# Pair sums by accumulating DMAs, all tap weights on GpSimd, the convolution on four array tiles

## The chip, the cores and the metric

The kernel runs on one core of a Trainium2 chip. The metric is device time in microseconds: 101.33 us before, the median of three runs (101.04 to 101.79). The five engines of a core are named as the profile names them: PE (TensorE, with PEld for its weight loads), DVE (VectorE), ACT (ScalarE), POOL (GpSimd) and SP (SyncE, which here only issues DMAs).

## What is computed

A deformable attention over four images of 64 channels and 32x32 pixels, then a binarized 3x3 convolution with batch norm, residual and PReLU:

```python
x = _L0_conv_ref(x, ...)   # deformable attention, + q
x = _L1_conv_ref(x, ...)   # binary convolution
# _L0: per pixel 8 heads x 4 points; attn = softmax(q @ W_attn + b_attn)
#      loc = ref + off / norm; bilinear samples of v = q @ W_value + b_value at loc
#      out = (sampled * attn).sum(points) @ W_out + b_out + q
# _L1: s = sign(x + move0); y = conv3x3(s, scale * sign(w)), scale = mean|w| per output channel
#      y = batchnorm(y) + x + move1; y = where(y >= 0, y, a*y) + move2
```

## The kernel before

The partition dimension holds two images of 64 channels (128 rows), and there are two such groups, `g` = 0 and 1. The pixels are split into an upper and a lower half (`yh`) of 512 pixels each. No gather is done. Each sampling point is near its own pixel, so the attention is a sum over 4x4 taps: for each of the 16 taps of each half (32 taps, `t` = 0..31; four taps of one vertical offset make a row, 8 rows), three engines work one after another:

- the weight of the tap, `ay * hat` (128x512): DVE makes it at L822 into `a`, or POOL at L738 into `ap`. `DVE_COLUMNS` says how many taps of a row are DVE's: 2 in row 0, 1 in every other row. DVE makes `ay` of a row in PSUM (`attend`, L813, behind taps 1, 3, 6, 10, 14, 18 and 22), and ACT copies it to SBUF (`copy_ay`, L611) for POOL, after DVE's own weight of that row is made.
- PE spreads the weight over channels (`spread(t)`, L420: four 64x64 tiles, f32, into one of two PSUM pairs). `spread(t)` waits for `product(t-2)`.
- DVE multiplies it with the shifted values (`product(t)`, L837, 128x1024, into slot `t % 8` of `prod`).

PE then projects the products into the output accumulators (`project`, L440, a "unit"). Taps 2 and 3 of each row are a unit each. Taps 0 and 1 are first added by POOL (`pair_sum`, L746, into `sum2`), so a row has three units, and row n's are put behind the spreads of row n+1 (`UNITS_AFTER`); the sum of row n stands behind `spread(4n+6)`, only sum 0 and sum 3 a group or two otherwise. `carry_x` (L433) adds x to the accumulators, before row 0's units and, for the lower half, behind `spread(20)`.

At the end PE runs the convolution: `convolve_row` (L469) issues for each of the 9 kernel positions and each group one 128x128 bf16 matmul with a block-diagonal weight over 512 pixels. The first three positions of group 0 stand ahead of the last unit, the rest of the upper half behind it. Then PE reads the flag that says whether an offset was out of range (a fallback branch, not taken here) and runs `convolve_rest`, which waits for the signs (L668, ACT) of the lower half: one pixel row of the upper half (128x32 matmuls) and the nine positions of the lower half, for each group in turn. DVE takes the statistics of each of the four PSUM banks (L938), then come the small steps of batch norm and the final elementwise work and four output DMAs.

## Time and profile before

| | us |
|---|---|
| median of three runs | 101.33 |
| the profiled execution | 101.12 |
| its span, first to last instruction | 99.2 |
| first spread to last spread | 16.4 to 76.4 |
| convolution and what stands between its parts | 78.2 to 87.5 |
| statistics, batch norm, final work, output | 87.5 to 99.2 |

Busy shares of the span are PE 81%, DVE 70%, POOL 56%, ACT 46%. The granted TensorE clock is at its full level until the convolution ends. A busy share is an average over these stages; so each stage is read by itself, from who waits for whom. Matmuls of different tiles start a few ns apart and overlap, so a group of four f32 matmuls on four tiles (8 records, since f32 takes two passes) shows about 1.06 us in the timeline but the next group starts 0.86 us after it.

### The profile page before, as it was taken

The numbers are of one execution on the slowest core, as the hardware profiler recorded it, in microseconds if no ns is written. First come the engines' busy times: TensorE is split into PE (matmuls) and PEld (weight loads), VectorE is DVE, ScalarE is ACT, GpSimd is POOL, SyncE is SP. The second block draws the span as 40 slices with busy tenths as digits, with TensorE's granted clock in tenths as the row PEclk, the third lists the DMA queues.
The fourth block names the chain that finished last, engine by engine and source line by source line (L and its number), as shares of the span: only waits on it lengthen the run. The fifth ranks groups of instructions, "written<-read, shape, count | busy, mean of one in ns | idle before, by whom it ended". The sixth has DMA issues, their size and how long they took to land.

```text
span 99.2 us, 1591 instructions
## 1 busy us (share of the span) xinstructions
PE 80.8 (81%) x598; PEld 32.7 (33%) x598; DVE 69.6 (70%) x89; ACT 45.8 (46%) x73; POOL 55.6 (56%) x42
## 2 busy tenths in 40 slices
PE   5999798698999785979979799979999999950000
PEld 4554281112344232324233345424242234420000
DVE  1405869989989930997994984998876434548990
ACT  3101999947999920099815590050000064003960
POOL 7950000189950899999999985984949000000600
PEclk9999999999999999999999999999999999999555
DMA  2997000000000000000000000000000000000055
GB/s 52 224 363 275 1 0 0 0 7 0 0 0 0 0 7 0 0 0 0 7 0 0 0 7 0 0 3 0 0 7 0 0 0 7 0 0 3 0 217 206
DMA packets 2169, 3.43 MB, mean 35 GB/s; under 512 B 368, under 2 KB 880, under 8 KB 2160
## 3 DMA queue, kind: packets, MB, share of 16 engines
q1 hardware_dynamic: 1872, 2.89, 8.5%
q10 hardware_dynamic: 288, 0.43, 1.8%
q8 instruction: 5, 0.08, 0.3%
q14 instruction: 4, 0.03, 0.1%
HBM read 2.27 MB, written 1.05 MB: 33 GB/s over the span
## 4 chain that ended last, share of the span: by engine, by line
PE 44%; issue 15%; ACT 13%; POOL 12%; DVE 12%; ACTq 1%; DVEq 0%; POOLq 0%
PE banks L420 14%; PE banks L440 11%; PE banks L469 8%; POOL ap L738 7%; DVE prod L837 5%; POOL sum L746 5%; ACT tab L599 4%; ACT hat L604 3%; PE banks L487 3%; DVE banks L813 2%; ACT prod L717 2%; PE banks L393 2%; PE banks L433 2%; PE banks L385 2%; ACT prod L719 1%
## 5 line engine op out<-in xcount | busy, mean ns | idle before, releaser
L837 DVE TENSOR_TENSOR prod<-banks,vpad 128x1024 f32<-128x1024 f32 (+1 forms) x33 | 38.5, 1186 | 11.2 <-PE banks L420 11.1
L738 POOL TENSOR_TENSOR ap<-ays,hat 128x512 f32<-128x512 f32 x23 | 28.9, 1290 | 13.7 <-ACT ays L611 13.7
L420 PE MATMUL banks<-ap,cst 64*64 64x512 f32 x184 | 26.0, 599 | 3.6 <-POOL ap L738 1.8
L746 POOL TENSOR_TENSOR sum<-prod 128x1024 f32<-128x1024 f32 x8 | 19.0, 2376 | 4.6 <-DVE prod L837 4.6
L440 PE MATMUL banks<-prod,wo 64*64 64x512 f32 x128 | 17.7, 591 | 0.0
L420 PEld LDWEIGHTS banks<-ap,cst 64*64 64x64 f32 x184 | 7.5, 132 | 16.4 <-issue 9.1
L611 ACT ACTIVATE ays<-banks 128x512 f32<-128x512 f32 x8 | 4.7, 592 | 15.0 <-DVE a L822 15.0
L420 PE MATMUL banks<-a,cst 64*64 64x512 f32 x72 | 10.2, 602 | 1.1 <-DVE prod L837 0.6
L770 POOL TENSOR_SCALAR prod<-prod,prm,st 128x512 f32<-128x512 f32 x2 | 1.5, 776 | 15.1 <-ACT st L711 15.1
L599 ACT ACTIVATE tab<-u,cst 128x1024 f32<-128x1024 f32 x8 | 8.9, 1141 | 0.2
L440 PE MATMUL banks<-sum,wo 64*64 64x512 f32 x64 | 9.0, 589 | 0.0
L440 PEld LDWEIGHTS banks<-prod,wo 64*64 64x64 f32 x128 | 6.0, 133 | 7.7 <-issue 7.1
L469 PE MATMUL banks<-sg,wcb 128*128 128x512 bf16 (+2 forms) x42 | 8.4, 352 | 0.0
L604 ACT ACTIVATE hat<-tab 128x1024 f32<-128x1024 f32 x8 | 8.3, 1047 | 0.1
L668 ACT ACTIVATE sg<-banks,st 128x512 bf16<-128x512 f32 x2 | 1.3, 688 | 14.3 <-PE banks L440 14.3
L822 DVE TENSOR_TENSOR a<-banks,hat 128x512 f32<-128x512 f32 x9 | 6.2, 692 | 0.3
L813 DVE TENSOR_TENSOR banks<-banks,hat 128x512 f32<-128x512 f32 x8 | 5.5, 691 | 0.8 <-PE banks L408 0.8
L469 PEld LDWEIGHTS banks<-sg,wcb 128*128 128x128 bf16 x42 | 3.5, 97 | 5.5 <-issue 1.6
L938 DVE BATCH_NORM_STATS2 bns<-banks 128x6 f32<-128x512 f32 x4 | 2.7, 695 | 3.3 <-PE banks L469 3.3
L420 PEld LDWEIGHTS banks<-a,cst 64*64 64x64 f32 x72 | 2.4, 131 | 7.3 <-issue 5.1
L440 PEld LDWEIGHTS banks<-sum,wo 64*64 64x64 f32 x64 | 3.0, 133 | 4.0 <-issue 3.4
L393 PEld LDWEIGHTS banks<-win,xs 128*128 128x128 f32 x32 | 3.8, 191 | 1.1 <-issue 1.1
(80 smaller groups left out, 83.1 us busy)
## 6 DMA issues: line engine op xcount, KB each, us to landing
out_dram<-prod SPq DMA_DIRECT2D x4, 256.0 KB, 2.1
xs<-x_dram SPq DMA_DIRECT2D x3, 256.0 KB, 5.1
wcf<-w_conv_dram SPq DMA_DIRECT2D x1, 288.0 KB, 5.4
wab<-w_abs_dram SPq DMA_DIRECT2D x1, 288.0 KB, 5.1
xs<-x_dram ACTq DMA_DIRECT2D x1, 256.0 KB, 4.0
cst<-const_dram SPq DMA_DIRECT2D x1, 227.0 KB, 5.3
win<-w_in_dram ACTq DMA_DIRECT2D x1, 160.0 KB, 2.6
cst<-const_dram SPq DMA_DIRECT2D x1, 128.0 KB, 5.7
```

What stands on the lines that cost most here:

```text
L393: mm = pe.matmul(ps_log[yh][:, at:at + C], xs[:, g, q:q + P], wp[:, 2, :], start=False, stop=(n == NCH - 1 and g == G - 1), skip_group_che ...
L420: mm = pe.matmul(ps_w[t % 2][rows_out, g, :], sel_of(g)[rows_in, rows_out], weights_at(t)[rows_in], start=True, stop=True)
L440: mm = pe.matmul(ps_out[g][rows_out], wo[rows_in, rows_in], source[rows_in, g, :], start=False, stop=last, skip_group_check=True)
L469: mm = pe.matmul(ps_y[yh][g][:, first_row * W:last_row * W], wcb[:, ky * K + kx, :], sg[:, g, y0:y0 + last_row - first_row, kx:kx + W], st ...
L599: nc.scalar.activation(tab[:, n % 2], u[:, :, yh, :], ACT.Abs, bias=cst[:, c_tap + k:c_tap + k + 1]).then_inc(s_abs, 1)
L604: nc.scalar.activation(hat[:, yh, :, k, :], tab[:, n % 2], ACT.Relu, bias=1.0, scale=-1.0).then_inc(s_hat, 1)
L611: nc.scalar.activation(ays[:, n % RY, :], ps_ay[:], ACT.Identity).then_inc(s_ayc, 1)
L738: pool.tensor_tensor(ap[:, j % RAP, :], ays[:, t // TAPS % RY, :], hat[:, yh, 0, kx, :], ALU.mult).then_inc(s_ap, 1)
L746: pool.tensor_tensor(sum2[:, n % NS], prod[:, t % PR], prod[:, (t + 1) % PR], ALU.add).then_inc(s_s2, 1)
L813: nc.vector.tensor_tensor(ps_ay[:], ps_att[:], hat[:, yh, 1, ORDER[row], :], ALU.mult).then_inc(s_ay, 1)
L822: nc.vector.tensor_tensor(a[:, i % RA, :], ps_ay[:], hat[:, yh, 0, kx, :], ALU.mult).then_inc(s_a, 1)
L837: nc.vector.tensor_tensor(by_half_row(prod[:, t % PR, g, :]), by_half_row(ps_w[t % 2][:, g, :]), v_window(g, yh, ky, kx), ALU.mult).then_i ...
```

## The change

- `DVE_COLUMNS` becomes 2 for row 0 and 0 for the others: POOL makes 30 weights rather than 23, DVE two rather than nine. `copy_ay` waits only for `attend`.
- `sum2` is gone. For rows 0 to 6 POOL issues a DMA that adds `prod` slot t+1 onto slot t (`accum_op=ALU.add`, 512 KB, SBUF to SBUF), with one semaphore for even and one for odd rows. The unit "sum n" waits for that DMA and reads the slot itself. `product(t+8)` for column 0 now waits until that unit is projected, for column 1 until the DMA has landed. Row 7 has no sum: its four taps are four units.
- `softmax_sum(1)` and `softmax_recip(1)` move from behind products 5 and 6 to behind products 3 and 4.
- `convolve_row` issues, for each position, four 64x64 bf16 matmuls on the four quadrants of the array (two images of each group at once), each with the 64x64 weight. `wcb` is 128x9x64, written by one activation rather than two, and its memset is gone. The two images of group 1 come out swapped, so its residual `x1` is stored swapped (four 64-partition copies on ACT), and each of its two output chunks is stored by two DMAs. Statistics of both groups wait for one semaphore per half.

```diff
-SUMMED = range(ROWS)
-DVE_COLUMNS = [2] + [1] * (ROWS - 1)
+SUMMED = range(ROWS - 1)
+DVE_COLUMNS = [2] + [0] * (ROWS - 1)
...
                 if kind == "sum":
-                    pe.wait_ge(s_s2, n + 1)
-                    source = sum2[:, n % NS]
+                    pe.wait_ge(s_s2[n % 2], 16 * (n // 2 + 1))
+                    source = prod[:, TAPS * n % PR]
...
-                    mm = pe.matmul(ps_y[yh][g][:, first_row * W:last_row * W], wcb[:, ky * K + kx, :],
-                                   sg[:, g, y0:y0 + last_row - first_row, kx:kx + W], start=(ky == 0 and kx == 0),
-                                   stop=(ky == K - 1 and kx == K - 1 and last_row == RH), skip_group_check=True)
+                    for g in range(G):
+                        for i in range(PAIR):
+                            rows_in, rows_out = quadrant(i, g)
+                            mm = pe.matmul(ps_y[yh][g][rows_out, first_row * W:last_row * W], wcb[rows_in, ky * K + kx, :],
+                                           sg[rows_in, g, y0:y0 + last_row - first_row, kx:kx + W], start=(ky == 0 and kx == 0),
+                                           stop=(ky == K - 1 and kx == K - 1 and last_row == RH), skip_group_check=True)
...
-            for g in range(G):
-                act.wait_ge(s_acc, UPPER_UNITS)
-                nc.scalar.activation(chunk(x1, g, 0), ps_out[g][:], ACT.Identity, bias=prm[:, p_bo:p_bo + 1]).then_inc(s_x1, 1)
-            act.wait_ge(s_zero, 4)
+            act.wait_ge(s_acc, UPPER_UNITS)
+            nc.scalar.activation(x1n[:], ps_out[1][:], ACT.Identity, bias=prm[:, p_bo:p_bo + 1]).then_inc(s_x1, 1)
+            nc.scalar.activation(chunk(x1, 0, 0), ps_out[0][:], ACT.Identity, bias=prm[:, p_bo:p_bo + 1]).then_inc(s_x1, 1)
+            act.wait_ge(s_zero, 3)
...
-                if n >= NS:
-                    pool.wait_ge(s_acc, units_done(("sum", n - NS)))
-                pool.tensor_tensor(sum2[:, n % NS], prod[:, t % PR], prod[:, (t + 1) % PR], ALU.add).then_inc(s_s2, 1)
+                pool.dma_start(prod[:, t % PR], prod[:, (t + 1) % PR], accum_op=ALU.add).then_inc(s_s2[n % 2], 16)
...
             for n in range(ROWS - 1):
-                weight(TAPS * (n + 1) + 1)
-                if n:
-                    pair_sum(n)
-                weight(TAPS * (n + 1) + 2)
-                weight(TAPS * (n + 1) + 3)
-                if n == 0:
-                    pair_sum(0)
+                for column in range(TAPS):
+                    weight(TAPS * (n + 1) + column)
+                    if column == 1:
+                        pair_sum(n)
...
-            pair_sum(ROWS - 1)
-
...
+                if t == 3:
+                    softmax_sum(1)
+                if t == 4:
+                    softmax_recip(1)
                 if t in ROW_AFTER:
                     n = ROW_AFTER.index(t) + 1
                     attend(n)
-                    weight(TAPS * n)
-                if t == 5:
-                    softmax_sum(1)
-                if t == 6:
-                    softmax_recip(1)
```

On POOL, at the start of the tap loop, these rows stood before (the products of the second half's softmax are `prob`; `sum` is the pair sum, `ap` the tap weights):

```order
L738 TENSOR_TENSOR ap<-ays,hat 128x512 x5
L746 TENSOR_TENSOR sum<-prod 128x1024
L760 TENSOR_TENSOR prob<-ex,lrec 128x512
L738 TENSOR_TENSOR ap<-ays,hat 128x512
L746 TENSOR_TENSOR sum<-prod 128x1024
L738 TENSOR_TENSOR ap<-ays,hat 128x512 x3
```

and these stand there now:

```order
L754 TENSOR_TENSOR ap<-ays,hat 128x512 x4
L760 DMA prod<-prod 128x1024
L754 TENSOR_TENSOR ap<-ays,hat 128x512 x2
L771 TENSOR_TENSOR prob<-ex,lrec 128x512
L754 TENSOR_TENSOR ap<-ays,hat 128x512 x2
L760 DMA prod<-prod 128x1024
L754 TENSOR_TENSOR ap<-ays,hat 128x512 x4
```

Each row of taps has four weights and a DMA where it had three weights and an add, and the first DMA is issued after four weights rather than five.

On PE, from the spread of tap 31 to the read of the flag, these rows stood before:

```order
L420 MATMUL banks<-ap,cst 64x512 x4
L440 MATMUL banks<-prod,wo 64x512 x4
L440 MATMUL banks<-sum,wo 64x512 x4
L469 MATMUL banks<-sg,wcb 128x512 x3
L440 MATMUL banks<-prod,wo 64x512 x4
L469 MATMUL banks<-sg,wcb 128x512 x3
L469 MATMUL banks<-sg,wcb 128x480 x3
L469 MATMUL banks<-sg,wcb 128x512 x6
L469 MATMUL banks<-sg,wcb 128x480 x3
L545 TENSOR_LOAD flagi
```

and these stand there now:

```order
L431 MATMUL banks<-ap,cst 64x512 x4
L451 MATMUL banks<-prod,wo 64x512 x12
L483 MATMUL banks<-sg,wcb 64x512 x12
L451 MATMUL banks<-prod,wo 64x512 x4
L483 MATMUL banks<-sg,wcb 64x512 x12
L483 MATMUL banks<-sg,wcb 64x480 x12
L556 TENSOR_LOAD flagi
```

Ahead of the convolution's first part stand three units (12 matmuls) rather than two. That part is three positions of both groups in 12 small matmuls, and behind the last unit 24 small matmuls stand where there were 15 large ones.

## Rows read from the trace of the kernel before

**Rows 1.** Timeline of PE, 33 to 76 us: start us, us, engine, line, operation [idle <-releaser].
```profile
33.07 1.11 PE L440 MATMUL banks<-prod,wo 64*64 64x512 f32 x6
35.00 1.09 PE L420 MATMUL banks<-ap,cst 64*64 64x512 f32 x8 [0.82 <-POOL ap L738]
...
38.53 1.09 PE L420 MATMUL banks<-ap,cst 64*64 64x512 f32 x8 [1.00 <-POOL ap L738]
...
43.59 1.09 PE L420 MATMUL banks<-ap,cst 64*64 64x512 f32 x8 [0.52 <-DVE prod L837]
44.47 1.07 PE L440 MATMUL banks<-prod,wo 64*64 64x512 f32 x8
45.33 1.07 PE L420 MATMUL banks<-ap,cst 64*64 64x512 f32 x8
...
75.52 1.04 PE L420 MATMUL banks<-ap,cst 64*64 64x512 f32 x8
```

**Rows 2.** Busy time by stretch: us, PE, PEld, DVE, ACT, POOL busy (x), PEclk, DMA.
```profile
35.00:75.70 40.70, 37.52 (x330) 14.65 (x334) 30.79 (x30) 13.77 (x31) 36.14 (x24) 1.00 0.01 2
```

**Rows 3.** Timeline of DVE around `attend` and the weight of a row.
```profile
40.90 0.69 DVE L813 TENSOR_TENSOR banks<-banks,hat 128x512 f32<-128x512 f32 x1
41.63 0.69 DVE L822 TENSOR_TENSOR a<-banks,hat 128x512 f32<-128x512 f32 x1
42.23 2.35 DVE L837 TENSOR_TENSOR prod<-banks,vpad 128x1024 f32<-128x1024 f32 x2
44.84 1.22 DVE L837 TENSOR_TENSOR prod<-banks,vpad 128x1024 f32<-128x1024 f32 x1 [0.26 <-PE banks L420]
```

**Rows 4.** Timeline of POOL, four places of the tap loop.
```profile
22.51 3.75 POOL L738 TENSOR_TENSOR ap<-ays,hat 128x512 f32<-128x512 f32 x3 [0.47 <-ACT ays L611]
...
32.60 1.10 POOL L760 TENSOR_TENSOR prob<-ex,lrec 128x512 f32<-128x512 f32 x1 [4.00 <-DVE lrec L791]
33.67 1.28 POOL L738 TENSOR_TENSOR ap<-ays,hat 128x512 f32<-128x512 f32 x1
...
60.63 2.36 POOL L746 TENSOR_TENSOR sum<-prod 128x1024 f32<-128x1024 f32 x1 [1.53 <-DVE prod L837]
```

**Rows 5.** Costliest groups: busy us, mean ns of one, idle before and its releaser.
```profile
L738 POOL TENSOR_TENSOR ap<-ays,hat 128x512 f32<-128x512 f32 x23 | 28.9, 1290 | 13.7 <-ACT ays L611 13.7
L746 POOL TENSOR_TENSOR sum<-prod 128x1024 f32<-128x1024 f32 x8 | 19.0, 2376 | 4.6 <-DVE prod L837 4.6
L611 ACT ACTIVATE ays<-banks 128x512 f32<-128x512 f32 x8 | 4.7, 592 | 15.0 <-DVE a L822 15.0
```

**Rows 6.** DMA queue of the loads and stores (packets, MB, share), and the output's issues.
```profile
q1 hardware_dynamic: 1872, 2.89, 8.5%
...
out_dram<-prod SPq DMA_DIRECT2D x4, 256.0 KB, 2.1
```

**Rows 7.** SP's DMA issues in the timeline: start us, us on SP, line, tensors, count.
```profile
3.06 0.43 SPq L359 DMA_DIRECT2D wo<-w_out_dram  x1
...
94.49 2.65 SPq L366 DMA_DIRECT2D out_dram<-prod  x4
```

**Rows 8.** The chain that ended last, from the convolution on: start us, us, what.
```profile
78.28 0.77 PE banks L469 x3
79.05 1.02 PE banks L440 x8
80.06 7.46 PE banks L469 x39
...
87.55 0.71 DVE bns L938
...
88.29 0.28 DVE mv L940
```

**Rows 9.** ACT's signs of the lower half, in its timeline.
```profile
80.16 1.27 ACT L668 ACTIVATE sg<-banks,st 128x512 bf16<-128x512 f32 x2 [14.33 <-PE banks L440]
```

**Rows 10.** By source line: PE's sequencer reads the flag, then goes on after the branch.
```profile
L545 PEldq TENSOR_LOAD <-flagi x1: 483/483/483, 80.0 to 80.0; - x1
...
L576 PEldq EVENT_SEMAPHORE  x1: 51/51/51, 81.3 to 81.3; - x1
```

**Rows 11.** Convolution alone, by stretch: us, PE busy (x), PEld busy (x), PEclk, DMA.
```profile
83.20:83.32 0.12, 0.12 (x5) 0.09 (x4) 1.00 0.00 0
```

More of the change, by code:

```diff
@@ L328, in units_of @@
             if n == ROWS - 1:
-                return [("tap", first + 2), ("sum", n), ("tap", first + 3)]
+                return [("tap", t) for t in range(first, first + TAPS)]
             return [("tap", first + 2), ("tap", first + 3), ("sum", n)]
         UNITS_AFTER = {6: [("tap", 2), ("tap", 3)], 7: [("sum", 0)], 17: [("tap", 15), ("sum", 3)], 18: [], 20: [],
-                       21: [("tap", 18), ("tap", 19)]}
+                       21: [("tap", 18), ("tap", 19)], 31: [("tap", 28), ("tap", 29)]}
         for n in range(2, ROWS):
@@ L568, in _ @@
                 pe.wait_ge(s_gs, 4)
[L569 to L571 removed]
+                for ky in range(K):
+                    convolve_above(ky)
             pe.end_ifs()
             pe.wait_ge(s_p, products_done(NT * YH - 1, G - 1))
[L575 to L577 removed]
+            pe.wait_ge(s_sg, 4)
+            convolve_rest()
             pe.wait_ge(s_mv, 1)
@@ L606, in copy_ay @@
             def copy_ay(n):
-                act.wait_ge(s_a, sum(DVE_COLUMNS[:n + 1]))
+                act.wait_ge(s_ay, n + 1)
+                if n == 0:
+                    act.wait_ge(s_a, DVE_COLUMNS[0])
                 if n >= RY:
@@ L693, in _ @@
                 sign(g, 1, ps_out[g][:], st[:, 16:17], s_sg)
+            for i in range(PAIR):
+                rows_in, rows_out = quadrant(i, 1)
+                nc.scalar.activation(chunk(x1, 1, 1)[rows_out], ps_out[1][rows_in], ACT.Identity,
+                                     bias=prm[rows_in, p_bo:p_bo + 1]).then_inc(s_x1swap, 1)
             act.wait_ge(s_flag, 1)
@@ L726, in _ @@
             pool.memset(vpad[:].rearrange("p g y a x -> p (g y a x)"), 0.0).then_inc(s_zero, 1)
-            pool.memset(wcb[:].rearrange("p k c -> p (k c)"), 0.0).then_inc(s_zero, 1)
             pool.memset(sg[:].rearrange("p g y x -> p (g y x)"), 0.0).then_inc(s_zero, 1)
@@ L877, in _ @@
             nc.vector.tensor_scalar(flagi[:], flag[:, 0:1], 0.0, None, ALU.is_gt).then_inc(s_flag, 1)
-            for g in range(G):
-                dve.wait_ge(s_sg, G + g + 1)
-                nc.vector.tensor_scalar(chunk(x1, g, 1), ps_out[g][:], prm[:, p_bo:p_bo + 1], None, ALU.add).then_inc(s_x1low, 1)
+            dve.wait_ge(s_sg, G + 1)
+            nc.vector.tensor_scalar(chunk(x1, 0, 1), ps_out[0][:], prm[:, p_bo:p_bo + 1], None, ALU.add).then_inc(s_x1low, 1)
             dve.wait_ge(s_flag, 1)
@@ L932, in _ @@
                         residual_of(yh, g, ps_gout[yh][g], s_gx)
+                dve.wait_ge(s_gx, 4)
+                dve.wait_ge(s_x1low, 1)
+                dve.wait_ge(s_x1swap, 4)
+                nc.vector.tensor_copy(x1[:, 0, :], gacc[:, 0, :]).then_inc(s_gn, 1)
+                for i in range(PAIR):
+                    rows_in, rows_out = quadrant(i, 1)
+                    nc.vector.tensor_copy(x1[rows_out, 1, :], gacc[rows_in, 1, :]).then_inc(s_gn, 1)
+                dve.wait_ge(s_gn, 3)
             dve.end_ifs()
             for n in range(G * YH):
-                g, yh = divmod(n, YH)
-                dve.wait_ge(s_y, n + 1)
+                yh, g = divmod(n, G)
+                dve.wait_ge(s_y, yh + 1)
                 nc.vector.bn_stats(bns[:, n, :], ps_y[yh][g][:]).then_inc(s_bns, 1)
```

92 lines of the change are left out of this document (50 added, 42 removed).

## The prediction

> **What bounds the kernel now.** I read the chain that ended last first, then the timelines of PE, DVE and POOL side by side. The chain runs through PE for most of its length, but in the tap loop it hops to DVE and POOL wherever PE waited. A group of four f32 matmuls starts 0.86 us after the one before it when nothing holds it (44.47 to 45.33 in [rows 1]). Between spread 9 (35.00) and spread 31 (75.52) the program has 39 such groups (22 spreads, 17 units), 1.72 for the carry of x, 0.62 for the transposes of the second softmax and 0.12 for the flag's matmul: 39 x 0.86 + 2.46 = 36.0 us of the 40.5. So 4.5 us are waits of PE. Twice it waits for a POOL weight (0.82 and 1.00 [rows 1]); four times (43.59 and three like it) it waits 0.5 to 0.6 for a product. The cause of the second kind is in [rows 3]: product 11 stands behind `attend` and DVE's own weight, 42.23 rather than 40.90. The cause of the first kind is in [rows 4]: POOL stood idle 4.00 us for the reciprocal and then had an add to do. Over the loop POOL is busy 36.1 of 40.7 us [rows 2], nearly as full as PE.
>
> **The tap loop up to spread 9.** POOL ends weight 3 at 22.0 as before. It then makes weights 4 and 5 (1.24 each: three in 3.75 [rows 4]), issues the first DMA at 24.5 and pays D for it, makes 6 and 7, `prob` (1.07) and 8 and 9. With D = 1.2, weight 9 is there at 31.8 instead of 34.95, the reciprocal having moved ahead. PE ends its previous group at 33.07 + 0.43 = 33.5 [rows 1], and the lower positions on ACT start 0.7 sooner since the copy of `ay` no longer waits for a DVE weight [rows 5]; spread 9 starts at about 33.4: **1.6 us sooner**.
>
> **From spread 9 to spread 31.** DVE loses seven weights; between product 10 and 11 there is `attend` alone, 0.62 us less. A spread must follow its predecessor but one by 1.24 to the product's start, 1.23 for the product and 0.13 back to PE, 2.60 in all, against 2.58 for three PE groups, so small waits stay: I take 0.28 a row, five rows, 1.4. That gives 33.4 + 36.0 + 1.4 = 70.8 for spread 31, **3.1 us more** on top, 4.7 in all. POOL's share: 22 weights and six DMA issues, 22 x 1.24 + 6D = 34.5 at D = 1.2, under 37.4, and it keeps ahead as far as the four weight buffers let it.
>
> **The accumulating DMA.** No row has one. Call T the time from POOL reaching it to its landing. It needs the product of column 1, thus about 2.5 us after that tap's spread (1.24 + 1.23 + 0.07), and the sum's unit stands ten groups behind that spread (8.6, and 0.3 of waits): T up to 6.4 costs nothing. Three places are tighter: sum 0 (issued 24.5, wanted 30.8: 6.3), sum 1 (issued 31.8 behind `prob`, wanted 36.8: 5.0), and sum 3, which stands one spread nearer (about 5.0 after POOL's issue). Stepping through the rows, the loop's end moves by 2(T - 5.0), and above 6.3 by another (T - 6.3), since then every row pays and each stall is half absorbed by the next. Bounds of T: the load and store queue moved 2.89 MB in 8.5% of 16 engines' span, 21.4 GB/s each, 343 together [rows 6]: 1.53 us for 512 KB in one pass, 3.06 if the destination is read besides. The output's 256 KB land 2.1 us after issue, 0.76 of it transfer [rows 6], so 1.35 is fixed. For D, an issue on SP holds it 0.43 [rows 7], the lower end, and I bound it above by the add it replaces, 2.37 [rows 5]. T lies between 0.43 + 1.35 + 1.53 = 3.3 and 2.37 + 1.35 + 4.6 = 8.3 (three passes). I take two passes and D = 1.2, between its ends: T = 5.6, which costs 1.2. Loop: 4.7 - 1.2 = **3.5 us gained**. The other bounds: 4.7, or with 8.3 a loss of 3.9.
>
> The Trainium skill (DMA: Bandwidth & Descriptors, "Anatomy of one DMA") fits a GpSimd-issued DMA by 2.0 us plus bytes over 436 GB/s, 3.2 us here; no run here shows one yet. By that alone the DMA would cost nothing and the total would be 1.2 us lower than mine.
>
> **The convolution and what leads to it.** Count from the end of spread 31, before at 76.38. Before: two units, three matmuls, the last unit ending 3.7 later (80.06), signs ready 1.37 after that [rows 9], the remaining 39 matmuls until 87.5, statistics until 88.3 [rows 8]: 11.9. After: three units (2.58), a switch (0.11), three positions, the last unit (1.09 to its end). The term to size is p, the time of a position in four small matmuls. A large matmul of 512 columns takes 0.215 (36 of about full length and six short ones in 0.77 + 7.46 us [rows 8]) and before a position takes two of them, 0.43. Four tiles at once take 0.215 if their matmuls overlap as those of L420 do. The upper bound is issue: that is eight instructions per position, and the f32 groups sustain 16 in 0.86, 0.43 per eight, without showing that they could go faster. Against that bound: five matmuls and four weight loads of 128x32 fit in 0.12 us [rows 11], so what is already queued runs faster than that. I take p = 0.27. Then the last unit ends at 2.58 + 0.11 + 0.81 + 1.09 = 4.6. The signs are ready at 6.0. The flag's read began when the remaining matmuls began, and the sequencer went on 1.29 later [rows 10]; with 24 small ones to hand out, partly ahead, I expect it 2.4 after the unit, 7.0. The rest is 12 short matmuls and nine positions, 0.6 + 2.4 = 3.0: 10.0. Now both lower banks end together, so two statistics of 0.65 stand behind, not one, and with the steps between the aggregate starts at 11.4 rather than 11.9: **0.5 us gained**. Ends: p = 0.215 with the signs as the limit (start at 5.9, 2.3 for the rest), 2.3 gained; p = 0.43 with everything bound by issue (last unit at 5.1, 2.6 to hand out the upper rest, about 1.1 for the branch, 48 pairs of 0.107, statistics), 15.3, 3.4 lost.
>
> **What costs nothing.** ACT's four swap copies (0.6 each): the upper two stand ahead of `copy_ay(6)`, whose weights are wanted over 5 us later; the lower two end 2.6 after the last unit, before batch norm wants them at about 7. If that cover went, each would cost its 0.6. The two extra output DMAs take 0.43 of SP each; the four chunks are issued in 2.65, 0.74 apart [rows 7], so a second half can push the next chunk by 0.1, and the last chunk, a single DMA with the widest gap ahead, is not delayed. The wcb memset and one activation go from engines that wait there.
>
> **The sum.** 3.5 + 0.5 = 4.0. The profiled execution took 101.12 (span 99.2 and 1.92 around it), 0.2 under the median: 101.12 - 4.0 = **97.1 us**.
>
> **Rivals.**
> - *The DMA lands late (slower).* T of 7.1 eats the gains of loop and tail (2 x 2.1 + 0.8 = 5.0, against 4.7 + 0.5), so from about 7.2 it decides; at 8.3 the loop loses 3.9, and 101.1 + 3.9 - 0.5 = **104.5**. For it: an addition has to read what it writes, and the queue's measured 21 GB/s an engine leaves 3.1 us for that alone. Against: it needs a third pass or a D of 2.4 besides.
> - *POOL becomes the bound.* If issuing takes D = 2.4, what the add took, POOL has 27.3 + 14.4 = 41.7 us between spread 9 and 31, and the DMA still has T over 5.2. That is 4.3 more than 37.4, and 1.2 more than the 40.5 of before: the loop keeps 0.4 of its 1.6 + 3.1, and with the tail's 0.5 the time is **100.2 us**. For it: POOL was busy 89% of the loop. Against: an issue on SP takes a sixth of it.
> - *The convolution is bound by issue.* The instruction count doubles for the same work. With p = 0.43 the tail loses 3.4: 101.1 - 3.5 + 3.4 = **101.0**, no change. For: nothing in the trace shows a faster sustained hand-out. The Trainium skill (TensorE: Matmul & The Clock Gate, Part 1) says the sequencer may spend about 62 ns per matmul and then binds once the array work per matmul is shorter; here that would be 53 ns, p = 0.25 if weight loads came free and 0.5 if they cost the same. The f32 groups' 107 ns per pair rules out the latter, and no row settles the former.
>
> **Chances.** The forecast, with T under 6.2 and p under 0.35: 0.50, its own range 94.1 (T = 5, p = 0.215) to 98.7. Late DMA 0.24. POOL bound 0.12. Issue bound 0.14. A change of 1% (about what a measurement here can tell) is 1.0 us. Faster: the forecast, half of the issue bound's (where p is short of 0.43) and half of POOL's: 0.63. Same: the other halves, 0.13. Slower: the late DMA's, 0.24. Range: 94.2 at the lower end; above, 103.0 leaves out half of the late DMA's chance.
>
> **What would show it.** Spread 31 starts near 72.0; before spread 9 no wait for POOL; PE's idle before L451 of a sum unit is under 1 us in total (if each row shows a wait for a DMA, the first rival); POOL's gap around its DMA issue is about 1.2; positions of L483 come 0.27 apart. The prediction is wrong if sum units wait every row, if weights on POOL are late again, or if the matmuls of L483 come one by one at over 0.1 us.

## The result, and the profile after

The changed kernel takes **95.68 us** (median of four runs, 95.59 to 96.38) against 101.19 for the kernel before on the same chip: ratio 0.9461, 95% interval 0.94 to 0.9521, so 5.5 us less. The prediction was 97.1, range 94.2 to 103.0. Medians here are over all executions of a kernel, and ratios leave out those more than 1.5% longer than its fastest. The profiled execution has a span of 93.9 us against 99.2.

Read the stages one by one. PE's timeline of the changed kernel (start us, us, engine, line, operation, count, idle before and who ended it); compare [rows 1] and [rows 8]:

```profile
16.69 1.09 PE L431 MATMUL banks<-a,cst 64*64 64x512 f32 x8 [0.29 <-DVE a L831]
...
33.35 1.34 PE L431 MATMUL banks<-ap,cst 64*64 64x512 f32 x8
...
52.19 1.09 PE L431 MATMUL banks<-ap,cst 64*64 64x512 f32 x8 [1.07 <-DVE prod L850]
...
71.42 1.04 PE L431 MATMUL banks<-ap,cst 64*64 64x512 f32 x8
72.28 2.76 PE L451 MATMUL banks<-prod,wo 64*64 64x512 f32 x24
74.86 0.84 PE L483 MATMUL banks<-sg,wcb 64*64 64x512 bf16 x12
75.52 1.04 PE L451 MATMUL banks<-prod,wo 64*64 64x512 f32 x8
76.38 1.46 PE L483 MATMUL banks<-sg,wcb 64*64 64x512 bf16 x24
78.07 2.27 PE L483 MATMUL banks<-sg,wcb 64*64 64x32 bf16 x48 [0.23 <-ACT sg L680]
82.03 0.38 PE L590 MATMUL banks<-mv,cst 128*128 128x2 f32 x2 [1.69 <-DVE mv L959]
```

The rows give a ledger that is used for every kernel below: first spread; from the first to the last spread (**loop**); from the end of the last spread, 0.86 after its start, to the matmuls on the aggregate (**tail**); from there to the end of the span (**output**).

| us | before | changed | gain |
|---|---|---|---|
| first spread at | 16.36 | 16.69 | -0.33 |
| loop | 59.16 | 54.73 | 4.43 |
| tail | 12.23 | 9.75 | 2.48 |
| output | 10.59 | 11.87 | -1.28 |
| span | 99.2 | 93.9 | 5.3 |

So two stages gave more than forecast (4.43 and 2.48, for 3.5 and 0.5), and one that was to cost nothing lost 1.3.

Who waits, in the list of waits of the changed kernel (engine, line, for whom: us in total, times, longest):

```profile
DVE prod L850 <- PE banks L431: 11.7, 17, 1.9
PEld banks L451 <- DMA prod<-prod: 1.1, 2, 0.8
PE banks L431 <- DVE prod L850: 1.1, 1, 1.1
```

DVE now waits for PE, not the reverse; the one long wait of PE for a product is that of spread 20 (52.19). The page of the changed kernel: POOL's weights, its DMA issues, the queue that they feed (packets, MB, share of 16 engines), and their landing (KB each, median us from issue), beside the output's:

```profile
L754 POOL TENSOR_TENSOR ap<-ays,hat 128x512 f32<-128x512 f32 x30 | 40.4, 1564 | 17.4 <-ACT ays L623 15.7
...
L760 POOL DMA_DIRECT2D prod<-prod x7 | 7.5, 1077 | 0.4 <-issue 0.4
...
q0 software_dynamic: 1008, 3.67, 20.6%
...
prod<-prod POOLq DMA_DIRECT2D x7, 512.0 KB, 4.8
...
out_dram<-prod SPq DMA_DIRECT2D x4, 128.0 KB, 2.6
out_dram<-prod SPq DMA_DIRECT2D x2, 256.0 KB, 2.6
```

The accumulating DMA lands 4.8 us after its issue (4.5 to 5.1). It shows 1.08 us on POOL, but part of it overlaps the next operation:

```profile
31.60 1.11 POOL L760 DMA_DIRECT2D prod<-prod  x1
32.21 5.51 POOL L754 TENSOR_TENSOR ap<-ays,hat 128x512 f32<-128x512 f32 x4
```

Here the next weight starts 0.61 after the issue, and behind the first of the seven 0.77, so that is what POOL pays: about a quarter of the add's 2.37 [rows 5].

### The profile page after: what moved, and what is told of

The parts are those of the page before. It is cut to its first block, busy times and chain, and to the rows that moved or that the text cites. A ratio compares the mean times of both kernels' runs of the same rounds, so it can differ in the third digit from the quotient of the medians.

```text
span 93.9 us, 1689 instructions
## 1 busy us (share of the span) xinstructions
PE 76.6 (82%) x648; PEld 33.0 (35%) x648; DVE 65.0 (69%) x81; ACT 47.9 (51%) x76; POOL 51.0 (54%) x47
## 3 DMA queue, kind: packets, MB, share of 16 engines
q0 software_dynamic: 1008, 3.67, 20.6%
HBM read 2.27 MB, written 1.05 MB: 35 GB/s over the span
## 4 chain that ended last, share of the span: by engine, by line
PE 67%; ACT 15%; DVE 7%; issue 4%; POOL 3%; ACTq 1%; DVEq 0%; POOLq 0%
PE banks L431 27%; PE banks L451 23%; PE banks L444 4%; ACT tab L609 3%; ACT hat L614 3%; PE banks L483 3%; PE banks L501 3%; POOL ap L754 2%; ACT prod L734 2%; PE banks L404 2%; PE banks L396 2%; ACT prod L736 2%; DVE bns L957 1%; ACT sg L680 1%; ACT u L602 1%
## 5 line engine op out<-in xcount | busy, mean ns | idle before, releaser
L754 POOL TENSOR_TENSOR ap<-ays,hat 128x512 f32<-128x512 f32 x30 | 40.4, 1564 | 17.4 <-ACT ays L623 15.7
L850 DVE TENSOR_TENSOR prod<-banks,vpad 128x1024 f32<-128x1024 f32 (+1 forms) x33 | 38.6, 1187 | 11.7 <-PE banks L431 11.7
L431 PE MATMUL banks<-ap,cst 64*64 64x512 f32 x240 | 33.9, 596 | 1.3 <-DVE prod L850 1.1
L451 PE MATMUL banks<-prod,wo 64*64 64x512 f32 x200 | 27.8, 590 | 0.0
L451 PEld LDWEIGHTS banks<-prod,wo 64*64 64x64 f32 x200 | 9.9, 133 | 11.5 <-issue 9.6
L760 POOL DMA_DIRECT2D prod<-prod x7 | 7.5, 1077 | 0.4 <-issue 0.4
L483 PE MATMUL banks<-sg,wcb 64*64 64x512 bf16 (+2 forms) x84 | 4.6, 350 | 0.2 <-ACT sg L680 0.2
L390 PE MATMUL banks<-xs,win 128*64 128x512 f32 x16 | 4.1, 611 | 0.0
L404 PE MATMUL banks<-win,xs 128*128 128x64 f32 x32 | 4.0, 277 | 0.0
L444 PE MATMUL banks<-xs,cst 64*64 64x512 f32 x16 | 3.8, 590 | 0.0
L396 PE MATMUL banks<-prm,top_ones 128*128 128x512 f32 x4 | 3.0, 846 | 0.7 <-ACT u L602 0.7
```

The source lines that it names most:

```text
L404: mm = pe.matmul(ps_log[yh][:, at:at + C], xs[:, g, q:q + P], wp[:, 2, :], start=False, stop=(n == NCH - 1 and g == G - 1), skip_group_che ...
L431: mm = pe.matmul(ps_w[t % 2][rows_out, g, :], sel_of(g)[rows_in, rows_out], weights_at(t)[rows_in], start=True, stop=True)
L444: mm = pe.matmul(ps_out[g][rows_of_i], cst[rows_of_i, c_eye + i * C:c_eye + (i + 1) * C], chunk(xs, g, yh)[rows_of_i], start=True, stop=Fa ...
L451: mm = pe.matmul(ps_out[g][rows_out], wo[rows_in, rows_in], source[rows_in, g, :], start=False, stop=last, skip_group_check=True)
L483: mm = pe.matmul(ps_y[yh][g][rows_out, first_row * W:last_row * W], wcb[rows_in, ky * K + kx, :], sg[rows_in, g, y0:y0 + last_row - first_ ...
L754: pool.tensor_tensor(ap[:, j % RAP, :], ays[:, t // TAPS % RY, :], hat[:, yh, 0, kx, :], ALU.mult).then_inc(s_ap, 1)
```

## The experiments

### Do the parts add up?

**Convolution alone**: the kernel before with the second half of the change. Core of the edit (the loop over two halves is for the chunks of group 1):

```diff
-            def convolve_row(yh, g, ky, first_row, last_row):
+            def convolve_row(yh, ky, first_row, last_row):
+                    for g in range(G):
+                        for i in range(PAIR):
+                            rows_in, rows_out = quadrant(i, g)
...
-                sp.dma_start(chunk_of(out, g, yh), chunk(res, g, yh)).then_inc(s_done, 16)
+                    for i in range(PAIR):
+                        rows_in, rows_out = quadrant(i, g)
+                        sp.dma_start(chunk_of(out, g, yh)[rows_in], chunk(res, g, yh)[rows_out]).then_inc(s_done, 16)
```

> The kernel before with the convolution on four tiles, the swap copies and the six output DMAs alone; its loop (adds on GpSimd, DVE's own weight) is unchanged. From the two traces, counted from the end of spread 31, the aggregate matmul came 2.5 us sooner after the change and the stretch behind it took 1.25 us longer. Theory A (the parts add up, and the longer output stage belongs to the six output DMAs): spread 31 starts at 75.5, the convolution gains 2.5, the output loses 1.2, and the time is 101.2 - 1.3 = 99.9 us; issues of the output DMAs take about 0.58 on SP. Theory B (the longer issues come from the accumulating DMAs of the loop, which share the 16 engines and leave something behind): here, without them, issues take 0.34 as before, the output loses nothing and the time is 98.7. Theory C (the convolution only gained because the loop freed GpSimd and ACT before it): gain 0.5 or less, 100.7 or more.

**Loop alone**: the kernel before with the first half, which is the DMAs, the weights on POOL, row 7 unsummed and the earlier softmax steps.

```diff
-SUMMED = range(ROWS)
-DVE_COLUMNS = [2] + [1] * (ROWS - 1)
+SUMMED = range(ROWS - 1)
+DVE_COLUMNS = [2] + [0] * (ROWS - 1)
...
-                pool.tensor_tensor(sum2[:, n % NS], prod[:, t % PR], prod[:, (t + 1) % PR], ALU.add).then_inc(s_s2, 1)
+                pool.dma_start(prod[:, t % PR], prod[:, (t + 1) % PR], accum_op=ALU.add).then_inc(s_s2[n % 2], 16)
```

> The kernel before with the new loop alone: pair sums by accumulating DMAs, all four weights of a row on GpSimd, the softmax sum sooner; convolution and four output DMAs as before. Theory A (parts add up): spread 31 starts at 71.4 as in the changed kernel, the convolution takes 11.9 from the end of spread 31 to the aggregate as before, the output issues take 0.34 and the output stage is that of before: 101.2 - 4.1 = 97.1 us. Theory B (the accumulating DMAs lengthen the output issues): issues take 0.58 although there are only four, and the time is 97.7 to 98.3.

Measured: 99.67 us (ratio 0.9838, 0.9802 to 0.9874) and 98.24 us (0.970, 0.967 to 0.973). PE's timelines of the two, last spread and aggregate, first of the convolution alone, then of the loop alone:

```profile
75.86 1.04 PE L433 MATMUL banks<-ap,cst 64*64 64x512 f32 x8
...
85.61 0.38 PE L593 MATMUL banks<-mv,cst 128*128 128x2 f32 x2 [1.70 <-DVE mv L964]
```

```profile
71.09 1.04 PE L418 MATMUL banks<-ap,cst 64*64 64x512 f32 x8
...
85.02 0.38 PE L577 MATMUL banks<-mv,cst 128*128 128x2 f32 x2 [1.09 <-DVE mv L935]
```

| us | first spread | loop | tail | output | span |
|---|---|---|---|---|---|
| before | 16.36 | 59.16 | 12.23 | 10.59 | 99.2 |
| convolution alone | 16.69 | 59.17 | 8.89 | 12.19 | 97.8 |
| loop alone | 16.36 | 54.73 | 13.07 | 11.28 | 96.3 |
| changed | 16.69 | 54.73 | 9.75 | 11.87 | 93.9 |

The loop is the same to 0.01 us with either convolution, and the new convolution shortens the tail by 3.34 behind the old loop too, so the theory that it gained only through a freer loop falls. The tail shows something that my expectation for the loop alone forgot, though the prediction had counted it: the new loop leaves the last row unsummed, which puts one more unit, 0.86, behind the last spread. The unit takes 0.84 to 0.86 of the 3.34 (12.23 to 8.89) back. The longer output comes with the six output DMAs: it is there in the convolution alone, where no accumulating DMA exists. The loop alone has 0.7 more too, of another kind: SP issues its four in 0.33 to 0.35 us each, as before the change, so the time is in theory B's range, but not for its reason. Its DMA view over the last 5.4 us, GB/s in 40 equal slices:

```profile
GB/s 0 0 0 0 0 0 197 379 410 349 394 364 410 379 364 394 364 425 349 410 364 243 15 182 440 394 334 425 152 15 15 30 15 15 0 0 0 0 0 0
```

Behind the last full slice stand five of 15 to 30 GB/s, one or two packets of 2 KB per slice, as if a single engine ended about 0.6 after the others. An instruction load (one packet, 0.01 MB) goes through the engines in that stretch. It does so in the output stretch of the changed kernel and of the one with whole chunks (below) too, which have no such end, so it doesn't explain it. The cause stays open.

### Which half of the loop's change gives the gain?

**GpSimd adds**: all four weights on POOL, but the sums by POOL's add.

```diff
...
-                pool.dma_start(prod[:, t % PR], prod[:, (t + 1) % PR], accum_op=ALU.add).then_inc(s_s2[n % 2], 16)
+                pool.tensor_tensor(sum2[:, n % NS], prod[:, t % PR], prod[:, (t + 1) % PR], ALU.add).then_inc(s_s2, 1)
```

> The changed kernel with the pair sums made by GpSimd's add again (2.37 us each), and still all four weights of a row on GpSimd. Theory A (GpSimd becomes the bound): from spread 9 to spread 31 it has 22 weights of 1.24 and 6 adds of 2.37, 41.5 us against the 38.1 that this stretch took, and a later start of spread 9 by about 1; the time is 95.7 + 4 = 99.7 us, so that the move of the weights pays only with the DMAs. Theory B (GpSimd has enough slack from its four weight buffers): 96.5 us or less.

**DVE column**: sums by DMA, but the first weight of a row on DVE, behind `attend`.

```diff
-DVE_COLUMNS = [2] + [0] * (ROWS - 1)
+DVE_COLUMNS = [2] + [1] * (ROWS - 1)
...
-                for column in range(TAPS):
+                for column in range(1, TAPS):
                     weight(TAPS * (n + 1) + column)
...
                     attend(n)
+                    weight(TAPS * n)
```

> The changed kernel with the first weight of each row on DVE as before (0.62 us each, seven of them) and the pair sums by DMA. Theory A (DVE's own weight is what made PE wait 0.5 to 0.6 a row): those waits come back in five rows, spread 31 starts about 2 us later than 71.4, 97.6 us. Theory B (GpSimd's relief, 1.24 a row, gives as much as DVE's load takes, or PE's waits had another cause): 95.4 to 96.2 us.

Measured: 99.26 us (ratio 0.979, 0.9741 to 0.9838) and 98.75 us (0.9733, 0.9686 to 0.978). POOL in the first, busy us from spread 9 to spread 31 (us, PE, PEld, DVE, ACT, POOL, clock, DMA share, GB/s):

```profile
34.66:75.06 40.40, 37.73 (x330) 13.19 (x326) 28.50 (x27) 14.78 (x32) 39.80 (x28) 1.00 0.01 2
```

39.8 of 40.4: with the adds, POOL is the bound. In the second, POOL has time but PE waits for products again, as in [rows 1]; three of the rows:

```profile
42.03 1.09 PE L431 MATMUL banks<-ap,cst 64*64 64x512 f32 x8 [0.52 <-DVE prod L848]
...
48.83 1.09 PE L431 MATMUL banks<-ap,cst 64*64 64x512 f32 x8 [0.52 <-DVE prod L848]
...
53.99 1.09 PE L431 MATMUL banks<-a,cst 64*64 64x512 f32 x8 [0.64 <-DVE prod L848]
```

| loop, us | first weight of a row on DVE | on POOL |
|---|---|---|
| sums by POOL | 59.16 | 58.25 |
| sums by DMA | 57.05 | 54.73 |

The upper left cell is the kernel before. The three others also have the softmax steps moved ahead and row 7 unsummed, and no run has these alone, so neither 0.9 nor 2.1 is the worth of one edit. By stretch, the four kernels take from the first spread to spread 9: 18.64 (before), 17.85 (GpSimd adds), 17.39 (DVE column) and 16.66 (changed). From spread 9 to spread 31 they take 40.52, 40.40, 39.66 and 38.07. So nearly all of the 0.9 lies at the start of the loop, where POOL had stood idle for the reciprocal [rows 4], and may be the softmax's. If moving the softmax costs nothing, what is left behind spread 9 bounds the edits: the weights alone give at most 0.1, the DMAs alone at most 0.9, both 2.45, and at least 1.5 is there only with both. A kernel with the softmax steps alone would settle it. The DMA makes room on POOL, and the weights use it to unload DVE. I had expected 1.1 less for the kernel with DVE's column: the waits came back as said, 1.6 us between spread 9 and spread 31, but spread 9 itself also came 0.95 later (34.30), only 0.22 of that because of a later first spread.

### The accumulating DMA: what it costs, and how much slack it has

**Plain copy**: the addition is left out.

```diff
-                pool.dma_start(prod[:, t % PR], prod[:, (t + 1) % PR], accum_op=ALU.add).then_inc(s_s2[n % 2], 16)
+                pool.dma_start(prod[:, t % PR], prod[:, (t + 1) % PR]).then_inc(s_s2[n % 2], 16)
```

> The changed kernel with its seven DMAs as plain copies of the same 512 KB, so the addition of the pair is left out. In the changed kernel such a DMA landed 4.5 to 5.1 us after its issue, held GpSimd about 0.6 to 0.75, and kept each engine busy for 2.76 us (20.6% of 93.9 us over seven). Theory A (an accumulating DMA reads what it writes, so the copy makes one pass instead of two): the copy takes about 1.4 to 1.6 us of the engines, lands after 3.4 to 3.7, PE's waits for it (1.1 us in two places) go, and the time is about 0.5 to 1 us less, 94.7 to 95.2. Theory B (the time is the fixed cost of a DMA that GpSimd issues): lands after 4.5 and the time stays at 95.7.

**Pair later**: the issue stands one weight further back on POOL.

```diff
-                    if column == 1:
+                    if column == 2:
                         pair_sum(n)
```

> The changed kernel with each pair sum issued behind the row's third weight on GpSimd instead of behind the second, 1.24 us later; so it lands 1.24 later wherever GpSimd is not waiting anyway. Theory A (the slack as the prediction put it: a landing up to 5.0 costs nothing, beyond it 2 us per us, since two sums are tighter than the rest): with 4.8 + 1.24 = 6.0 the loop gets 2 us longer, 97.7, and PE waits for the DMA in two or three places only. Theory B (PE runs close behind the DMA in every row): the wait appears in all seven rows and costs 1 us each, 100 or more. Theory C (there is slack everywhere, and GpSimd gains from not waiting for the product): 95.4 to 96.0.

Measured: the copy 95.52 us (ratio 0.9404, 0.9376 to 0.9432), the later pair 98.33 us (0.9701, 0.9649 to 0.9754). The page of the copy, its queue and its landing:

```profile
q0 software_dynamic: 1008, 3.67, 9.7%
...
prod<-prod POOLq DMA_DIRECT2D x7, 512.0 KB, 2.9
```

For the same 512 KB the engines work 9.7% x 93.3 / 7 = 1.29 us a copy and 20.6% x 93.9 / 7 = 2.76 us an accumulation, and the landing goes from 2.9 to 4.8. So an accumulation costs the engines a little over twice the copy, as the prediction's second pass would. The Trainium skill (DMA: Bandwidth & Descriptors, "Anatomy of one DMA") gives 3.2 us for a GpSimd-issued DMA of this size; the copy's 2.9 is near it, the accumulation's 4.8 is not, so that fit does not hold for `accum_op`. And the 1.9 us are worth almost nothing here: the loop is 54.58 with the copy and 54.73 with the addition. The 1.1 us of waiting for the DMA in the list above are PEld's, whose weight loads run ahead of the matmuls; PE itself has no wait for a DMA. The one place where the matmuls are held back is the sum of row 3, the DMA that took 5.1 to land. The two units of that place, in the changed kernel and then with the copy:

```profile
47.34 2.07 PE L451 MATMUL banks<-prod,wo 64*64 64x512 f32 x16
```

```profile
47.00 1.93 PE L451 MATMUL banks<-prod,wo 64*64 64x512 f32 x16
```

The spread behind them starts 1.89 and 1.72 after their start, so the wait costs 0.17, which is the loop's 0.15. It isn't taken up by the next stall: the wait before spread 20 is 1.07 and 1.06.

Issued later, the same DMA costs 2.1 us: loop 56.83. The waits:

```profile
PEld banks L451 <- DMA prod<-prod: 5.3, 6, 1.7
...
PE banks L451 <- DMA prod<-prod: 1.6, 3, 0.8
```

and PE stops before three sums, 0.49, 0.79 (here) and 0.29 us:

```profile
49.87 1.09 PE L451 MATMUL banks<-prod,wo 64*64 64x512 f32 x8 [0.79 <-DMA prod<-prod]
```

With the issue 1.24 further back, T goes from 4.8 to about 6.0. The prediction's slack rule, nothing up to 5.0 and 2 us per us beyond, gives 2.1; measured 2.1 in the loop. (The profiled span rose 2.1 as well, the median time 2.65; no trace shows the other 0.5.) Theory A holds, and with it a warning: the change sits on the knee, with the sum of row 3 landing at 5.1 and already costing its 0.17.

### The wait before spread 20

**Sum of row 3 later**: a unit goes between spreads 18 and 19.

```diff
-        UNITS_AFTER = {6: [("tap", 2), ("tap", 3)], 7: [("sum", 0)], 17: [("tap", 15), ("sum", 3)], 18: [], 20: [],
+        UNITS_AFTER = {6: [("tap", 2), ("tap", 3)], 7: [("sum", 0)], 17: [("tap", 15)], 18: [("sum", 3)], 20: [],
```

> The changed kernel with one unit moved: the sum of row 3 is projected after spread 18 and not after spread 17. In the changed kernel three spreads (18, 19, 20) stood without a unit between 18 and 19 and after 20, and PE waited 1.07 us for DVE's product before spread 20 (52.19). Theory A (PE's order makes the stall: a spread must stand 2.6 us behind its predecessor but one, and two groups take 1.7): with the unit between, the wait goes and spread 31 starts 0.9 to 1.1 sooner, 94.7 us. Theory B (DVE is the limit over the loop, so a stall removed at one place returns at the next): gain below 0.3, 95.4 to 95.7.

Measured 95.21 us (ratio 0.9379, 0.9342 to 0.9415); spans 93.0, 92.6, 92.8, 92.8 against 93.9, 94.0, 93.8, 93.9. The same spread in PE's timeline:

```profile
51.38 1.09 PE L431 MATMUL banks<-ap,cst 64*64 64x512 f32 x8 [0.20 <-DVE prod L850]
```

The wait of 1.07 is 0.20, and the loop 53.71: 1.02 less. The wait was made by PE's order, and it didn't return elsewhere. The median time fell by only 0.47, since more of it lies outside the span (1.9 to 2.8 us a run, against 1.8 to 2.4 in the changed kernel); the intervals of the two ratios overlap, the spans don't.

### The output stage

Three kernels change who issues the output, one changes what is issued.

**Half on ACT**: SP issues one half of chunk (1,1), ACT the other. **Split chunk last**: the same, with the order of the last two chunks turned, so that ACT waits for the fourth result (`wait_ge(s_res, 4)`); the last two lines are its alone.

```diff
-                    for i in range(PAIR):
+                    for i in range(PAIR if n == 0 else 1):
...
+            act.wait_ge(s_res, 3)
+            rows_in, rows_out = quadrant(1, 1)
+            act.dma_start(chunk_of(out, 1, 1)[rows_in], chunk(res, 1, 1)[rows_out]).then_inc(s_done, 16)
...
-            return yh, G - 1 - k
+            return yh, G - 1 - k if yh == 0 else k
```

> The changed kernel with one of the six output DMAs (the second half of chunk (1,1)) issued by ACT, so that SP has five. In the changed kernel SP issued six DMAs back to back at 87.92, 88.49, 89.12, 89.75, 90.26 and 90.90, and the last was ready to go at about 90.24. Theory A (SP's queue of issues delays the last one): the last issue moves from 90.90 to about 90.3 and the time falls by 0.6, to 95.1. Theory B (the last landing is set by something else, 2.6 us after its issue rather than 2.1, since the small descriptors of the halves stand ahead of it in the same engines): the time falls by 0.2 or less.

> The changed kernel with the last two chunks of the result in the other order, so that the split chunk is last, and its two halves issued by SP and by ACT at the same time. Theory A (halves on two queues go through the 16 engines side by side and use all ports, so a split chunk costs what a whole one costs): whole chunk issued at about 89.8, halves both at about 90.3, last packet at about 92.5 instead of 93.17, time 95.0 us. Theory B (the engines work through one DMA after another, whichever queue): within 0.2 of the changed kernel, 95.5 to 95.9.

**Halves by GpSimd** (with the sum of row 3 later; SP leaves out the first split chunk):

```diff
+            pool.wait_ge(s_res, 1)
+            for i in range(PAIR):
+                rows_in, rows_out = quadrant(i, 1)
+                pool.dma_start(chunk_of(out, 1, 0)[rows_in], chunk(res, 1, 0)[rows_out]).then_inc(s_early, 16)
```

> The kernel with the sum of row 3 one spread later (95.2 us, span 92.6 to 93.0), and with the first split chunk of the output issued by GpSimd, which is idle by then, so that SP has four issues. Putting one half on ACT's queue brought 0.1 in one order of the chunks and cost 0.6 in another. Theory A (the six DMAs follow one another at about 0.7 us because of the hardware queue that SP feeds, and GpSimd's queue runs beside it): the whole chunk is issued at 87.8 rather than 88.3, the last packet comes 0.5 to 0.8 sooner, 94.5 us. Theory B (the 16 engines are shared and a half costs its 0.7 whoever issues it): 95.1 to 95.4. [...]

**Whole chunks**: each split chunk goes out in one DMA. It leaves out the exchange of the two images, so the images of group 1 stay swapped in the output.

```diff
-                    for i in range(PAIR):
-                        rows_in, rows_out = quadrant(i, g)
-                        sp.dma_start(chunk_of(out, g, yh)[rows_in], chunk(res, g, yh)[rows_out]).then_inc(s_done, 16)
+                    sp.dma_start(chunk_of(out, g, yh), chunk(res, g, yh)).then_inc(s_done, 16)
```

> The changed kernel with the chunks of the swapped images written by one DMA of 128 partitions each instead of two of 64, so four output DMAs; the exchange back of the two images of a pair is left out. In the kernel with the new loop alone the output DMAs were whole and SP issued them in 0.33 to 0.35 us each, in those with the new convolution in 0.47 to 0.60. With one of six moved to ACT the last issue on SP came 0.68 earlier and the last packet only 0.10 earlier, so the issue on SP is not what ends last; the packets of a half took 144 ns against 89. Theory A (a DMA over half the partitions is slow in itself, in issue and per packet): with whole DMAs the issues return to 0.34, from the first issue to the end it takes 4.7 us as in the kernel before instead of 6.0, and the time is 95.7 - 1.3 = 94.4 us. Theory B (the output stage is longer for another reason, such as results that are written by engines in another order): 95.3 or more.

Measured:

| | us | ratio (interval) | output |
|---|---|---|---|
| changed | 95.68 | 0.9461 (0.94 to 0.9521) | 11.87 |
| row 3 later | 95.21 | 0.9379 (0.9342 to 0.9415) | 11.77 |
| half on ACT | 95.56 | 0.9427 (0.9393 to 0.9461) | 11.82 |
| split chunk last | 96.28 | 0.9503 (0.9424 to 0.9581) | 12.36 |
| halves by GpSimd (row 3 later) | 95.92 | 0.9443 (0.9395 to 0.9492) | 12.54 |
| whole chunks | 94.48 | 0.9337 (0.9267 to 0.9408) | 10.61 |

Only whole chunks bring the output stage back to the 10.59 of before. SP's issues in the changed kernel (start us, us, tensors, count), then with whole chunks:

```profile
87.92 1.16 SPq L377 DMA_DIRECT2D out_dram<-prod  x2
89.12 0.58 SPq L373 DMA_DIRECT2D out_dram<-prod  x1
89.75 1.11 SPq L377 DMA_DIRECT2D out_dram<-prod  x2
90.90 0.58 SPq L373 DMA_DIRECT2D out_dram<-prod  x1
```

```profile
87.97 0.35 SPq L375 DMA_DIRECT2D out_dram<-prod  x1
88.64 0.38 SPq L373 DMA_DIRECT2D out_dram<-prod  x1
89.30 0.33 SPq L375 DMA_DIRECT2D out_dram<-prod  x1
90.29 0.33 SPq L373 DMA_DIRECT2D out_dram<-prod  x1
```

and over the last 6.0 us of the changed kernel and the last 4.8 of that with whole chunks, in 40 slices each, the busy share of the 16 engines in tenths and GB/s:

```profile
DMA  0100000169988999599997787999799987000000
GB/s 0 55 0 0 0 0 0 41 177 218 218 178 219 218 191 218 137 355 382 396 341 260 273 273 219 259 259 232 232 301 382 382 328 273 27 0 0 0 0 0
```

```profile
DMA  0000100389999899999998999218999960000000
GB/s 0 0 0 0 68 0 0 119 307 444 324 341 427 308 359 410 358 375 393 359 444 341 444 358 358 86 51 341 375 410 375 393 222 17 0 0 0 0 0 0
```

While only halves are under way (the first nine full slices) the engines move about 180 to 220 GB/s, with whole chunks 310 to 440, and they are busy in most slices of both. So it is not the number of DMAs or gaps between them that cost: a half carries 128 KB in nearly the time of 256. That is why it doesn't matter who issues it: with one half on ACT, SP's last issue came at 90.22 instead of 90.90, but the landing of its whole chunks went from 2.6 to 3.0 us, and next to nothing was gained. Two halves side by side on two queues (split chunk last) brought nothing either, and with GpSimd's halves SP's chunks landed 3.3 and 3.4 us after their issue, not 2.5; that output stage is 12.54 against 11.77 for the same kernel without it. The Trainium skill (SBUF — State Buffer, "Door 1: The DMA port swizzle") says why a half is so slow: partitions 0 to 63 reach 8 of 16 ports, for at most about 218 GB/s, and all 128 reach 436. This trace agrees, with 177 to 219 for the halves and up to 444 for whole chunks. It also says (DMA: Bandwidth & Descriptors, "Rules for kernel authors") that two transfers to disjoint partition halves serialize and that spreading over SP, ACT and GpSimd does not help, since all use the same 16 engines. The split chunk last agrees in the outcome: its two halves were issued together at 90.55 on two queues, ACT's landed 3.8 us later, and the output took 12.36. GB/s over its last 6.5 us:

```profile
GB/s 0 0 0 50 0 0 0 139 227 202 202 177 227 202 189 177 378 391 391 366 265 365 353 328 252 176 139 101 177 252 391 189 114 51 25 13 0 0 0 0
```

The last halves reach 391 GB/s in one slice, so for a moment they did run side by side, and then the last packets came in at 114 down to 13. Why they straggle is open, and the turned order of the chunks wasn't run by itself.

**Both edits**: row 3's sum later and one half on ACT.

```diff
-        UNITS_AFTER = {6: [("tap", 2), ("tap", 3)], 7: [("sum", 0)], 17: [("tap", 15), ("sum", 3)], 18: [], 20: [],
+        UNITS_AFTER = {6: [("tap", 2), ("tap", 3)], 7: [("sum", 0)], 17: [("tap", 15)], 18: [("sum", 3)], 20: [],
...
-                    for i in range(PAIR):
+                    for i in range(PAIR if n == 0 else 1):
...
+            act.dma_start(chunk_of(out, 1, 1)[rows_in], chunk(res, 1, 1)[rows_out]).then_inc(s_done, 16)
```

> The two edits of the changed kernel that each brought a little, together: the sum of row 3 one spread later, and the second half of chunk (1,1) issued by ACT. The first took about 1 us off the span (93.0, 92.6, 92.8, 92.8 against 93.9, 94.0, 93.8, 93.9), the second 0.15 (93.8, 93.5, 94.0, 93.7). Theory A (both hold and add, as they lie in stages apart): span 92.4 to 92.9, time 94.4 to 95.1, and the interval of the ratio lies below that of the changed kernel, 0.946. Theory B (the edit of the order only moves a wait, and its gain was that of a few executions): span 93.6 and over, 95.5.

Measured **94.99 us** over six runs, ratio 0.9378 (0.933 to 0.9426), spans 92.5 to 93.0: 0.7 us under the changed kernel. The intervals of the two ratios just overlap, the spans don't (93.8 to 94.0 in the changed kernel). Nearly all of it is the order's, whose kernel has spans of 92.6 to 93.0; the half on ACT can't be told from nothing.

## Why the prediction was right in sign, and where its sizes came from

- **Up to spread 9: right, with some luck.** 1.6 sooner was forecast for 33.4, and it stands at 33.35. With the first spread of before it would stand at 33.0: the stretch gave 2.0, and the later start hid the other 0.4.
- **Spread 9 to 31: right, 0.5 us too cautious.** The forecast was 36.0 of work, 1.4 of small waits and 1.2 for the DMA, 38.6; measured 38.07. The step that was too dear is the DMA's: T was taken as 5.6 from two passes and D = 1.2, measured 4.8 (5.1 for the sum of row 3) and D = 0.6 to 0.8, at the knee of 5.0, and worth 0.15 in the loop as the plain copy shows. The slack rule itself held at T = 6.0. The small waits were too cheap instead, 2.1 less 0.15 against 1.4, of which the one before spread 20 alone is 1.07. The forecast spread the same 0.28 over all rows; the order of units in the code would have shown this place.
- **The rivals late DMA and POOL bound did not come.** The first needed T over 7.2. The second needed POOL at 41.7 us of work; it had 31.3 from spread 9 to 31. It does come true with the adds on POOL (39.8 of 40.4).
- **The convolution: the gain was five times the forecast, 2.5 for 0.5.** The step that failed is "I expect it 2.4 after the unit, 7.0", the start of the rest. It started 5.8 after the end of spread 31, released by the signs, not by the hand-out:

```profile
76.65 1.27 ACT L680 ACTIVATE sg<-banks,st 128x512 bf16<-128x512 f32 x2 [14.92 <-PE banks L451]
```

  The signs end at 77.92 and the matmuls follow at 78.07, while by source line the flag was read at 76.0, before the 24 upper matmuls had even begun:

```profile
L556 PEldq TENSOR_LOAD <-flagi x1: 483/483/483, 76.0 to 76.0; - x1
```

  The forecast hung the start on the sequencer's branch, counted from when the remaining matmuls began. Here the flag was read 2.1 before the start, and with the 1.29 that the branch took before [rows 10] the sequencer was through at about 77.3, an estimate, ahead of the signs at 77.92. The signs came 0.36 sooner than its own 6.0. Mistaken too was p. Twelve small matmuls take 0.84 us and 24 take 1.46, 0.052 each, 0.21 a position instead of 0.27. Three positions ahead of the last unit, nine behind the signs and the signs as the limit are the lower end of my bounds, which gave 2.3. In numbers, the start of the rest gave 1.2 more than forecast and its length 0.7 (2.27 for 3.0). The remaining 0.3 up and 0.3 down are a slip of the prediction, whose 11.9 for before ends with the statistics (88.3) while its 11.4 ends with the aggregate (88.6 before, 12.2), and the statistics after, 1.7 for its 1.4. The rows show 52 ns for a small matmul with its weight load, where the rival bound by issue needed 107 (p = 0.43), so it falls. The Trainium skill (TensorE: Matmul & The Clock Gate, Part 1) gives the sequencer about 62 ns a matmul with hardware decode off; the trace is below that, so this price did not apply here.
- **The output: wrong.** "The two extra output DMAs ... can push the next chunk by 0.1, and the last chunk ... is not delayed" took a half as a small DMA. It costs nearly as much as a whole one, on the engines and on SP, and the stage lost 1.3. The port rule of the Trainium skill cited above spoke against that line and I had not weighed it: a half at 218 GB/s takes as long as a whole at 436, by its figures 0.6 us, so the two extra DMAs would be an estimated 1.2 us, close to the 1.28 lost.
- **The sum.** Forecast 3.5 + 0.5 + 0 = 4.0; measured 4.43 + 2.48 - 1.28 - 0.33 = 5.3 in span. Against the forecast the loop gave 0.9 more (0.4 of it ahead of spread 9) and the tail 2.0 more; the output took 1.3 back and the first spread 0.3. So the time came out 1.4 under the forecast, well inside its own range of 94.1 to 98.7. Part of that is luck: errors of opposite sign partly cancelled, and without the loss at the output and the later start the time would have been 94.1, at the very end of the range.
- **The 0.33 at the start** was at nothing in the forecast. Part of it is the change's: in all twelve kernels with the new convolution PE waits 0.66 or 0.67 for ACT's `u` ahead of the tap loop, and 0.53 in the two with the old one, before and then changed:

```profile
11.56 1.10 PE L385 MATMUL banks<-prm,top_ones 128*128 128x512 f32 x2 [0.53 <-ACT u L592]
```

```profile
11.89 1.10 PE L396 MATMUL banks<-prm,top_ones 128*128 128x512 f32 x2 [0.67 <-ACT u L602]
```

  The rest varies: the first matmuls on x begin at 6.18 in the two old ones and anywhere from 6.05 (plain copy, first spread at 16.36 like before) to 6.66 in the others (first spread 16.66 to 16.98). The cause of either part wasn't looked for.

## What to carry to other kernels

When two engines are both nearly full, free the one that can take the other's work: here, from spread 9 on, the kernel with only the weights moved gained 0.1, that with only the DMAs 0.9, that with both 2.45 (all three with the softmax steps moved too). Before an operation is handed to a slow asynchronous path, count the slack of each consumer, not the mean: 4.8 us cost 0.15, 1.24 us more cost another 2.1. And don't price a split transfer by its bytes; a DMA over half the partitions cost nearly a whole one, so a layout that needs such halves at the end of a kernel pays for them in full.

## What the hardware showed that was not expected

- An accumulating DMA within the chip's own memory, 512 KB over 128 partitions: 4.8 us from issue to landing and 2.76 us of each engine, against 2.9 and 1.29 for the copy.
- A whole output chunk is issued by SP in 0.33 to 0.38 us as long as no half has gone before it on SP; behind one it takes 0.45 to 0.79. With the first halves issued by GpSimd, SP's first whole chunk took 0.35 and the one behind SP's own halves 0.59:

```profile
87.87 0.35 SPq L374 DMA_DIRECT2D out_dram<-prod  x1
88.47 1.16 SPq L378 DMA_DIRECT2D out_dram<-prod  x2
89.67 0.59 SPq L374 DMA_DIRECT2D out_dram<-prod  x1
```

  Why isn't settled.
- In the loop alone the last output packets came one or two of 2 KB at a time, about 0.6 us after the rest; the cause is open.
- Four 64x64 tiles with bf16 data hold 52 ns per matmul of 512 columns with a weight load each, so four of them take 0.21 us, what one matmul of 512 columns on a 128x128 tile takes (0.215).
